# Fusing two layer norms, a SiLU and the output sum into one loop over token tiles, and taking out a run of dummy matmuls

## What is computed

```python
xn = _layernorm(x, axis=-1)
s = _L0_attn_ref(xn, ...)         # causal attention, 16 heads, then its own layer norm:
                                  #   y = o @ Wo + bo
                                  #   (y - mu) * rsqrt(var + 1e-5) * gamma + beta
g = _silu(_L0_ffn_ref(xn, ...))   # six nodes; node c: q, k, v from earlier nodes, 8-head attention,
                                  #   nodes[c] = act_w[c] * o + q
                                  #   then _layernorm(nodes[5], ln_g, ln_b) with 1e-6
x = x + s * g
return x
```

## Time and profile before

| what | us |
|---|---|
| median of 3 runs | 7834.37 (7825.6 to 7962.15) |
| the profiled execution's own time | 7835.35 |
| its span, first to last instruction of the slowest core (core 3) | 7833.8 |
| spans of the 8 cores | 7763.3 to 7833.8 |
| TensorE busy in the span | 5975.0 |
| VectorE busy | 2200.5 |
| ScalarE busy | 2734.2 |
| GpSimd busy | 365.8 |

### The profile page before, as it was taken

How to read it: one execution, slowest core, us unless ns; L and a number is a source line. 1 busy time by engine, 2 the same in 40 slices (tenths; PEclk the granted TensorE clock), 3 DMA queues, 4 the chain that set the end, 5 groups by cost and what they waited for, 6 DMA issues and landing times.

```text
span 7833.8 us, 62633 instructions; the slowest of 8 cores (7763.3 to 7833.8 us)
## 1 busy us (share of the span) xinstructions
PE 5975.0 (76%) x21971; PEld 1965.7 (25%) x21971; DVE 2200.5 (28%) x3068; ACT 2734.2 (35%) x2612; POOL 365.8 (5%) x355
## 2 busy tenths in 40 slices
PE   6677797777987779877789777897777878778830
PEld 2322233222332223322234222342222311111110
DVE  3133321333113332133321333213332122222155
ACT  0155432544225442155431454214552123333301
POOL 0100011000010000100011000110001100000000
PEclk9989898888998889988899888998888955555665
DMA  2300032000420004200033000230003100000013
GB/s 75 103 1 1 6 102 65 1 1 30 113 73 0 1 17 113 87 0 1 1 88 105 0 1 1 81 110 3 1 1 92 54 0 0 1 0 0 1 46 105
DMA packets 204570, 289.40 MB, mean 37 GB/s; under 512 B 141576, under 2 KB 141800, under 8 KB 204268
## 3 DMA queue, kind: packets, MB, share of 16 engines
q1 hardware_dynamic: 204236, 285.39, 12.7%
q0 software_dynamic: 32, 0.00, 0.0%
HBM read 218.24 MB, written 33.55 MB: 32 GB/s over the span
## 4 chain that ended last, share of the span: by engine, by line
PE 67%; DVE 18%; issue 6%; ACT 4%; DMA 4%; SPq 1%; DVEq 1%; POOL 0%; ACTq 0%; POOLq 0%
PE ps L395 17%; PE ps L575 9%; PE ps L880 8%; DVE attb L626 6%; PE ps L636 6%; PE ps L645 5%; PE ps L458 5%; PE ps L621 5%; DVE stat L526 4%; PE ps L606 3%; PE ps L597 3%; PE ps L519 3%; DVE attb L510 2%; DMA fio<-x 2%; ACT attb L686 1%
## 5 line engine op out<-in xcount | busy, mean ns | idle before, releaser
L686 ACT ACTIVATE attb<-ps,negM,scal 128x1024 bf16<-128x1024 f32 x1536 | 1765.9, 1198 | 1934.5 <-DVE negM L542 1433.5
L395 PE MATMUL ps<-slot,wbuf 128*128 128x512 bf16 x6144 | 1367.2, 383 | 99.5 <-POOL wbuf L369 75.5
L575 PE MATMUL ps<-qbuf,kbuf 128*128 128x512 bf16 x3072 | 1027.4, 425 | 172.1 <-ACT attb L686 149.3
L626 DVE TENSOR_TENSOR attb<-attb 128x1024 bf16<-128x1024 bf16 x768 | 537.9, 700 | 1788.3 <-PE ps L621 1772.0
L395 PEld LDWEIGHTS ps<-slot,wbuf 128*128 128x128 bf16 x6144 | 604.4, 99 | 848.7 <-issue 139.5
L880 PE MATMUL ps<-slot,wbuf 128*128 128x512 bf16 x3072 | 692.2, 384 | 84.0 <-POOL wbuf L369 84.0
L636 PE MATMUL ps<-attb,ones_bf 128*1 128x512 bf16 x1536 | 476.6, 392 | 360.6 <-DVE attb L626 354.3
L519 PE MATMUL ps<-attb,ones_sq 128*128 128x512 bf16 (+1 forms) x512 | 237.4, 561 | 610.2 <-DVE attb L510 608.9
L369 POOL CAST wbuf<-wstage 128x1024 bf16<-128x1024 f32 x344 | 363.3, 1060 | 5759.4 <-DVE kbuf L891 3653.7
L686 ACT ACTIVATE attb<-ps,negM 128x1024 bf16<-128x1024 f32 (+7 forms) x384 | 327.7, 862 | 665.8 <-PE ps L575 664.2
L621 PE MATMUL ps<-attb,slot 128*128 128x512 bf16 x1536 | 497.1, 408 | 19.6 <-DVE slot L748 19.6
(11 more groups left out here) (104 smaller groups left out, 2701.4 us busy)
## 6 DMA issues: line engine op xcount, KB each, us to landing
wstage<-fWe SPq DMA_DIRECT2D x120, 512.0 KB, 4.3
wstage<-fWv SPq DMA_DIRECT2D x48, 512.0 KB, 4.2
wstage<-fWq SPq DMA_DIRECT2D x48, 512.0 KB, 4.3
wstage<-fWk SPq DMA_DIRECT2D x48, 512.0 KB, 4.3
wstage<-fWo SPq DMA_DIRECT2D x48, 512.0 KB, 4.3
slot<-n_sp SPq DMA_DIRECT2D x40, 512.0 KB, 8.5
fio<-x SPq DMA_DIRECT2D x32, 512.0 KB, 4.2
n_sp<-slot SPq DMA_DIRECT2D x32, 512.0 KB, 2.7
```

The lines of the kernel that those rows point to most:

```text
L395: t.matmul(ps[pb][:, sg * SEG:(sg + 1) * SEG], wtile(ws, kc, do * 128, 128), fchunk(ss, kc, th * TW + sg * SEG, SEG), start=(kc == 0), sto ...
L575: t_s = P.op("tensor", lambda t, kc=kc, sg=sg, pb=pb: t.matmul(ps[pb][:, sg * PSEG:(sg + 1) * PSEG], kf_tile_fn(kc), q_rhs_fn(sg * PSEG, P ...
L626: t_pr = P.op("vector", lambda v, a0=a0, a1=a1: v.tensor_tensor(attb[a0][:, 0:PW], attb[a0][:, 0:PW], attb[a1][:, 0:PW], ALU.add), waits=[ ...
L686: off=off: s.activation(attb[ab][:, off:PW], ps[pb][:, off:PW], AF.Exp, bias=negM[:, nc_:nc_ + 1], scale=scale_col),
```

## The change

Two edits. The 72 dummy matmuls and the fill ahead of them go. And the end is rewritten: both parameter pairs are built first, the second one into `gamT2`, which is the free weight staging tile `wstage[0]` read as bf16. Then one loop over the 16 token tiles does everything: layer norm of y, layer norm of the graph's result, `Silu`, the product, the sum and the write. The arithmetic for each tile is the same, operation by operation. The transposes of a tile pair are issued by `issue_T`, two tiles ahead, into four tiles `attb[0..3]` with a semaphore each. The diff, cut to its core (what is left out of `ln_tile` is the arithmetic of `ln_apply_loop` with other buffer numbers):

```diff
-WARM_N = 72
...
     ps_last[1] = t_scal
-
-    t_wrm = P.op("gpsimd", lambda g: g.memset(lrow[0:1, 0:1024], 1.0),
-                 inc="tPOOL")
-    for wj in range(WARM_N):
-        P.op("tensor", lambda t: t.matmul(
-            ps[0][:, 512:1024], ones_f32r[0:1, :], lrow[0:1, 0:512],
-            start=True, stop=True),
-            waits=[t_wrm, t_on2] if wj == 0 else [], inc="tPE")
...
-    def build_gam(i0, i1, ready):
+    gamT2 = wstage[0].ap().bitcast(BF16)
+
+    def build_gam(i0, i1, ready, dst_fn, wgate=()):
         toks = []
         for j, i in enumerate((i0, i1)):
             tr = P.op(trq, lambda g, i=i: g.dma_start(
                 out=lrow[0:1, 0:1024], in_=W[vps[4 + i]].ap()[None, :]),
                 waits=pser() + list(ready) + toks, inc="P", inc_n=16)
...
                 te = P.op("vector", lambda v, j=j, h2=h2: v.tensor_copy(
-                    gamT[:, j * 1024 + h2 * 512: j * 1024 + (h2 + 1) * 512],
-                    ps[3][:, h2 * 512:(h2 + 1) * 512]), waits=[tm], inc="tDVE")
+                    dst_fn(j, h2), ps[3][:, h2 * 512:(h2 + 1) * 512]),
+                    waits=[tm] + list(wgate), inc="tDVE")
                 ps_last[3] = te
                 toks.append(te)
         return toks
...
-    def ln_apply_loop(dst_slot, src_sp, src_ready, eps, gam_toks):
-        toks = []
-        for tc in range(TC):
-            b = tc % 2
-            tk = P.op(trq, lambda g, tc=tc, b=b, a=src_sp: g.dma_start(
-                out=attb[b][:, 0:1024], in_=a.ap()[:, tc * 128:(tc + 1) * 128],
-                transpose=True),
-                waits=list(src_ready) + attb_free[b], inc=f"T{b}", inc_n=16)
-            q0 = 8 + b * 4
...
-            t10 = P.op("vector", lambda v, b=b, ds=dst_slot, tc=tc:
-                       v.tensor_tensor(
-                tchunk(ds, tc), attb[b][:, 0:1024], gamT[:, 1024:2048],
-                ALU.add), waits=[t9], inc="tDVE")
-            attb_free[b] = [t10]
-            slot_written(dst_slot, tc % max(KC, TC), t10)
-            toks.append(t10)
-        return toks
+    def ln_tile(dst_slot, eps, g0, g1, tc, ab, psb, q0, tk):
+        t1 = P.op("vector", lambda v, ab=ab, q0=q0: v.reduce_sum(
...
+    def ln_tile(dst_slot, eps, g0, g1, tc, ab, psb, q0, tk):
+        t1 = P.op("vector", lambda v, ab=ab, q0=q0: v.reduce_sum(
+            stat[:, q0:q0 + 1], attb[ab][:, 0:1024], axis=AX.X),
+            waits=[tk], inc="tDVE")
+        t4 = P.op("vector", lambda v, ab=ab, q0=q0, psb=psb:
+                  v.scalar_tensor_tensor(
+            ps[psb][:, 0:1024], attb[ab][:, 0:1024], 1.0,
+            attb[ab][:, 0:1024], ALU.mult, ALU.mult,
+            accum_out=stat[:, q0 + 1:q0 + 2]),
+            waits=[tk, ps_last[psb]], inc="tDVE")
+        ps_last[psb] = t4
...
+        t10 = P.op("vector", lambda v, ab=ab, g1=g1, ds=dst_slot, tc=tc:
+                   v.tensor_tensor(
+            tchunk(ds, tc), attb[ab][:, 0:1024], g1,
+            ALU.add), waits=[t9], inc="tDVE")
+        attb_free[ab] = [t10]
+        slot_written(dst_slot, tc % max(KC, TC), t10)
+        return t10
 
     fio_free[2] = ps_last[2]
-    gam_s = build_gam(0, 1, y_spills)
-    s_toks = ln_apply_loop(Dv, y_sp, y_spills, 1e-5, gam_s)
-    gam_g = build_gam(2, 3, s_toks)
-    g_toks = ln_apply_loop(B, n5_sp, n5_spills, 1e-6, gam_g)
-    gs_toks = []
-    for tc in range(TC):
-        gs_toks.append(P.op("scalar", lambda s, tc=tc: s.activation(
-            tchunk(B, tc), tchunk(B, tc), AF.Silu), waits=[g_toks[tc]],
-            inc="tACT"))
-
+    gam_s = build_gam(0, 1, y_spills, lambda j, h2: gamT[
+        :, j * 1024 + h2 * 512: j * 1024 + (h2 + 1) * 512])
+    gam_g = build_gam(2, 3, list(n5_spills) + gam_s, lambda j, h2: gamT2[
+        :, j * 1024 + h2 * 512: j * 1024 + (h2 + 1) * 512],
+        wgate=[wstage_free[0]])
+    fio_free[2] = gam_g[-1]
+
+    tkS, tkG = {}, {}
+
+    def issue_T(tc):
+        if tc >= TC:
+            return
+        b = tc % 2
+        tkS[tc] = P.op(trq, lambda g, tc=tc, b=b: g.dma_start(
+            out=attb[b][:, 0:1024], in_=y_sp.ap()[:, tc * 128:(tc + 1) * 128],
+            transpose=True),
+            waits=list(y_spills) + attb_free[b] + gam_s,
+            inc=f"T{b}", inc_n=16)
+        tkG[tc] = P.op(trq, lambda g, tc=tc, b=b: g.dma_start(
+            out=attb[2 + b][:, 0:1024],
+            in_=n5_sp.ap()[:, tc * 128:(tc + 1) * 128], transpose=True),
+            waits=list(n5_spills) + attb_free[2 + b] + gam_g,
+            inc=f"T{2 + b}", inc_n=16)
+
+    issue_T(0)
+    issue_T(1)
     out_toks = []
     for tc in range(TC):
         b = tc % 2
+        s_tok = ln_tile(Dv, 1e-5, gamT[:, 0:1024], gamT[:, 1024:2048],
+                        tc, b, b, b * 4, tkS.pop(tc))
+        g_tok = ln_tile(B, 1e-6, gamT2[:, 0:1024], gamT2[:, 1024:2048],
+                        tc, 2 + b, 2 + b, 8 + b * 4, tkG.pop(tc))
+        gs_tok = P.op("scalar", lambda s, tc=tc: s.activation(
+            tchunk(B, tc), tchunk(B, tc), AF.Silu), waits=[g_tok],
+            inc="tACT")
+        issue_T(tc + 2)
...
         tx = P.op(pln, lambda g, tc=tc, b=b: g.dma_start(
             out=fio[b][:, :], in_=x_in.ap()[tc * 128:(tc + 1) * 128, :]),
             waits=[fio_free[b]], inc=f"X{b}", inc_n=16)
         t1 = P.op("vector", lambda v, tc=tc: v.tensor_tensor(
             fio[2][:, :], tchunk(Dv, tc), tchunk(B, tc), ALU.mult),
-            waits=[s_toks[tc], gs_toks[tc], fio_free[2]], inc="tDVE")
+            waits=[s_tok, gs_tok, fio_free[2]], inc="tDVE")
         t2 = P.op("vector", lambda v, b=b: v.tensor_tensor(
             fio[2][:, :], fio[2][:, :], fio[b][:, :], ALU.add),
             waits=[tx, t1], inc="tDVE")
```

More of the change, by code:

```diff
@@ L1038, in build_gam @@
             for h2 in range(2):
-                tm = P.op("tensor", lambda t, j=j, h2=h2: t.matmul(
+                tm = P.op("tensor", lambda t, h2=h2: t.matmul(
                     ps[3][:, h2 * 512:(h2 + 1) * 512], ones_f32r[0:1, :],
@@ L1109, in build_nc @@
-    fio_free[2] = ps_last[2]
-    gam_s = build_gam(0, 1, y_spills)
-    s_toks = ln_apply_loop(Dv, y_sp, y_spills, 1e-5, gam_s)
-    gam_g = build_gam(2, 3, s_toks)
-    g_toks = ln_apply_loop(B, n5_sp, n5_spills, 1e-6, gam_g)
-    gs_toks = []
-    for tc in range(TC):
-        gs_toks.append(P.op("scalar", lambda s, tc=tc: s.activation(
-            tchunk(B, tc), tchunk(B, tc), AF.Silu), waits=[g_toks[tc]],
-            inc="tACT"))
+    def ln_tile(dst_slot, eps, g0, g1, tc, ab, psb, q0, tk):
[9 more added lines that the diff above has]
+        ps_last[psb] = t4
+        tm = P.op("vector", lambda v, q0=q0: v.tensor_scalar(
+            stat[:, q0:q0 + 1], stat[:, q0:q0 + 1], 1.0 / D, None,
+            ALU.mult), waits=[t1], inc="tDVE")
+        tq = P.op("vector", lambda v, q0=q0: v.tensor_tensor(
+            stat[:, q0 + 2:q0 + 3], stat[:, q0:q0 + 1],
+            stat[:, q0:q0 + 1], ALU.mult), waits=[tm], inc="tDVE")
+        tv = P.op("vector", lambda v, q0=q0: v.tensor_scalar(
+            stat[:, q0 + 1:q0 + 2], stat[:, q0 + 1:q0 + 2], 1.0 / D,
+            None, ALU.mult), waits=[t4], inc="tDVE")
+        tv = P.op("vector", lambda v, q0=q0: v.tensor_tensor(
+            stat[:, q0 + 1:q0 + 2], stat[:, q0 + 1:q0 + 2],
+            stat[:, q0 + 2:q0 + 3], ALU.subtract),
+            waits=[tv, tq], inc="tDVE")
+        tv = P.op("vector", lambda v, q0=q0, eps=eps: v.tensor_scalar(
+            stat[:, q0 + 1:q0 + 2], stat[:, q0 + 1:q0 + 2], 1.0, eps,
+            ALU.mult, ALU.add), waits=[tv], inc="tDVE")
+        t6 = P.op("scalar", lambda s, q0=q0: s.activation(
+            stat[:, q0 + 2:q0 + 3], stat[:, q0 + 1:q0 + 2], AF.Ln),
+            waits=[tv], inc="tACT")
+        t7 = P.op("scalar", lambda s, q0=q0: s.activation(
+            stat[:, q0 + 1:q0 + 2], stat[:, q0 + 2:q0 + 3], AF.Exp,
+            scale=-0.5), waits=[t6], inc="tACT")
+        t7 = P.op("vector", lambda v, q0=q0: v.tensor_tensor(
+            stat[:, q0 + 3:q0 + 4], stat[:, q0:q0 + 1],
+            stat[:, q0 + 1:q0 + 2], ALU.mult), waits=[t7], inc="tDVE")
+        t8 = P.op("vector", lambda v, ab=ab, q0=q0: v.tensor_scalar(
+            attb[ab][:, 0:1024], attb[ab][:, 0:1024],
+            stat[:, q0 + 1:q0 + 2], stat[:, q0 + 3:q0 + 4],
+            ALU.mult, ALU.subtract), waits=[t7], inc="tDVE")
+        t9 = P.op("vector", lambda v, ab=ab, g0=g0: v.tensor_tensor(
+            attb[ab][:, 0:1024], attb[ab][:, 0:1024], g0,
+            ALU.mult), waits=[t8], inc="tDVE")
+        t10 = P.op("vector", lambda v, ab=ab, g1=g1, ds=dst_slot, tc=tc:
[5 more added lines that the diff above has]
+        return t10
```

## The result

The changed kernel's median is 7874.91 us in 11 runs, that of the kernel before 7834.76 us beside it. The ratio of the two, from their comparable runs, is 1.0039 with a 95% interval of 1.0026 to 1.0052: slower by 31 us, between 20 and 41, and so within 2%. The forecast was 7876 us, +40.5 us; by the ratio the change costs 31.

What follows compares the result with a forecast made beforehand. TensorE was taken to bound the body; the fused end, VectorE's in-order list with late x, sums 201.8 + 19.4 + 109.2 + 10.2 + 3.05 = 343.7 us against 303.2, +40.5, giving 7876 us; range 7838 to 7908.

Steps and rivals of the forecast that it cites:

- The body: 7206.5 us from the first projection on, bound by TensorE; the change leaves every instruction in it where it was.
- the ramp of the clock: First projection's start: about a dozen matmuls at 0.43 us, as before; dummy matmuls' removal worth 0, bounds -1 and +3 us.
- D: Body: without its early load TensorE is granted a lower clock; slower by over 2%, 8046 us; chance 0.04.
- The mark that was set for it: Forecast is wrong if the body's stretch differs by more than 20 us between the profiles.
- Parameter pairs: Before the new loop: two pairs, each 15.4 us, now stand behind each other; effect 0.
- The period: New loop: a tile every 21.7 us, the last two about 19; no product waits for the write.
- The tables: y norms but the first: VectorE waits 1.29 us more for the `Ln` table load, 19.4 us; bounds 0 and 38.7.
- rival A: ScalarE in the new loop: a table switch costs more than its load, 21.8 us more, 7898 us; chance 0.09.
- x decides over `Silu`: New loop's sum: x lands 6.5 us after the norm, 2.7 us behind the `Silu` path; 109.2 us in 14 tiles.
- the other end of the bound: x load in the new loop: landing in 4.2 us, the middle one of all loads, makes the end 14 us less.
- B: New loop: x doesn't arrive last, so the `Silu` path decides; 305.9 us, +2.7 us, total 7838; chance 0.07.
- C: New loop: table loads done while ScalarE idles and x early; 16.4 us a tile, -38 us, 7798; chance 0.02.

Runs made afterwards that it cites:

- the first experiment: Only the 72 dummy matmuls taken out of the kernel before; ratio to that kernel 1.0005, interval 0.9984 to 1.0026.
- the fifth run: Changed kernel plus a one-element `Ln` behind each `Silu` and a one-element `Silu` behind the n5 norm's `Exp`; no ratio, tiles 312.75 us on core 5.
- the third run: Changed kernel with each tile's x load issued ahead of the two transposes; ratio to the kernel before 1.0011, tiles 307.8 us on core 1.

## Why the prediction was right, point by point

**The body.** Predicted to stay; no change of it can be seen (7265.8 against 7269.3 us on the cores read), and the ramp of the clock is no longer either. The rival that the missing early load reaches into the body (D) fell with the first experiment. The mark that was set for it, 20 us between the profiles, was too fine for single cores, which differ by up to 67 us within one execution; the medians over the cores are what shows it.

**Parameter pairs.** 0 predicted; 30.4 us against twice 15.4.

**The period.** A tile was to take 21.7 us, the last two about 19. The first fourteen take 20.96 in the mean (from 7528.65 to 7822.02), the one after them 19.03, and no wait for the write is left.

**The tables.** 15 x 1.29 = 19.4 us predicted. The wait for the statistics rose by 18.8, and taking it away gave 20. The row at 35.53 of the trace before, with a load that starts when the data are there and not when the engine is free, decided this rightly. The rule of the Trainium skill ("ScalarE: Activation LUTs", What ACT_TABLE_LOAD costs) with a drain of another 1.38 us, and rival A with it, does not hold here: the wait grew by 1.97 - 0.69 = 1.28 us, the load alone, and in the run with product and sum one tile late a load stands 0.02 us behind a finished `Silu` and takes the same 1.28.

**x decides over `Silu`.** Right: the fifth run moved 20 us from one wait to the other and the time stayed, and the third took the wait for x away by order alone. The size was off, and this is the mis-sized term of the sum: x was taken to land 5.2 us after its issue, from the one load that stood behind a transpose, which made the sum's wait 2.7 us and the term 109.2 us. Measured is a landing of 4.4 us (the middle one of 16) and a wait of 28.9 / 14 = 2.06 us. That is 14 x 0.64 = 9 us, which accounts for the 8.75 by which the predicted 343.7 us exceed the measured 334.95. DMA issues in the new loop, core 1:

```profile
fio<-x SPq DMA_DIRECT2D x16, 512.0 KB, 4.4
```

The 4.2 us over all loads, which stood as the other end of the bound, was the somewhat better guide: with it the sum gives 329.7 us, 5.3 too few, and the time 7862. One transfer is a poor sample.

**The rivals.** B (x early) needed a landing in 2.5 us and C (a gain) an early x too, which none of the fourteen loads behind transposes showed. But their mechanisms could be built: the third run is B, at 307.8 us for the tiles where 305.9 was worked out; the small activations take both table loads off the path, which is C, at 268.0 where 265 was worked out.

## What to carry to other kernels

Putting loops into one overlaps nothing by itself, where each engine runs a list in order. What counts is what stands ahead of each load in its queue, and what each engine still has to do while it would otherwise wait; here one moved line was worth 27 us, and with x early, both small activations and each tile finished behind the next tile's norms the end of the fused kernel is 55 us shorter than that of separate loops, where plain fusing had made it 31 us longer. Of that the late finish by itself is worth 19 us (268.0 to 248.8); what it would give without the small activations was not run. Where functions with different tables alternate, a one-element activation in a pause takes the load off the path, but first look whether that path is the later one. Dummy matmuls were worth nothing where TensorE idled behind them, for 2.4 us or for 77.
